# Layer 0's attention: ScalarE squares three of the 22 units of each group of heads a second time itself

## What is computed

```python
def polynomial_attention(q, k, v, degree, is_causal):       # degree = 4
    a = jnp.einsum('bhnd,bhmd->bhnm', q, k) ** degree
    if is_causal:
        a = jnp.tril(a)
    denom = jnp.sum(a, axis=-1, keepdims=True)
    return jnp.einsum('bhnm,bhmd->bhnd', a / denom, v)
```

## Time and profile before

| | us |
|---|---|
| median of 3 runs | 889.47 |
| lowest, highest | 888.18, 890.79 |
| the profiled execution's own time | 884.85 |
| its span, first to last instruction | 883.1 |
| this stage in it, first score to last `read_out0` | 207 to 318 |

### The profile page before, as it was taken

How to read it: one execution, slowest core, us unless ns; L and a number is a source line. 1 busy time by engine, 2 the same in 40 slices (tenths; PEclk the granted TensorE clock), 3 DMA queues, 4 the chain that set the end, 5 groups by cost and what they waited for, 6 DMA issues and landing times.

```text
span 883.1 us, 13675 instructions
## 1 busy us (share of the span) xinstructions
PE 798.7 (90%) x4707; PEld 632.4 (72%) x4707; DVE 621.6 (70%) x1115; ACT 447.9 (51%) x795; POOL 426.8 (48%) x474
## 2 busy tenths in 40 slices
PE   2999999988888866998899899999999999999996
PEld 2866666664223345777889788989999998887874
DVE  8377767458898855888895996767776655555556
ACT  3322231168666723476654656655666653555541
POOL 2466736334655533554532456676773310655550
PEclk9999999997787796999999999999999999999999
DMA  5121195000000004000000001110110477654307
GB/s 176 36 72 36 37 280 134 1 0 1 1 1 1 1 1 140 14 19 12 19 7 19 7 20 42 44 48 25 49 49 14 169 165 283 200 145 114 89 4 236
DMA packets 50114, 59.79 MB, mean 68 GB/s; under 512 B 13559, under 2 KB 41084, under 8 KB 50048
## 3 DMA queue, kind: packets, MB, share of 16 engines
q1 hardware_dynamic: 45488, 50.49, 19.1%
q0 software_dynamic: 4560, 8.44, 2.7%
HBM read 41.11 MB, written 21.86 MB: 71 GB/s over the span
## 4 chain that ended last, share of the span: by engine, by line
PE 71%; DVE 17%; issue 4%; ACT 4%; POOL 3%; DMA 0%; SPq 0%; DVEq 0%; ACTq 0%; POOLq 0%
PE ps L693 11%; PE ps L452 11%; PE ps L454 11%; PE ps L453 10%; PE ps L778 7%; PE ps L596 6%; PE ps L802 3%; DVE A L1245 3%; PE ps L533 2%; DVE swap L1309 2%; DVE cap L1319 2%; PE ps L516 2%; PE ps L491 2%; PE ps L759 2%; DVE qk_tok L1245 1%
## 5 line engine op out<-in xcount | busy, mean ns | idle before, releaser
L693 PE MATMUL ps<-V,P 128*128 128x129 f32 x1152 | 152.8, 279 | 0.0
L993 ACT ACTIVATE cap<-cap 128x1024 f32<-128x1024 f32 (+7 forms) x128 | 87.1, 680 | 123.6 <-DVE cap L1319 117.2
L693 PEld LDWEIGHTS ps<-V,P 128*128 128x128 f32 x1152 | 145.4, 194 | 2.7
L1319 DVE SCALAR_TENSOR_TENSOR cap<-dist,ps 128x1024 f32<-128x1024 f32 (+7 forms) x128 | 95.1, 749 | 25.6 <-PE ps L454 20.7
L1528 POOL TENSOR_SCALAR_AFFINE_SELECT P<-P 128x128 f32<-128x128 f32 x128 | 38.6, 302 | 149.5 <-ACT P L998 149.2
L1653 POOL DMA_INDIRECT y_scratch<-y_sb,aux_s x63 | 62.0, 984 | 64.5 <-issue 35.2
L998 ACT ACTIVATE P<-cap 128x1024 f32<-128x1024 f32 (+7 forms) x128 | 87.7, 685 | 4.1
L452 PE MATMUL ps<-q_hi,k_hi 128*128 128x512 f32 x192 | 72.2, 376 | 6.5 <-DVE cap L1319 6.2
L1245 DVE TENSOR_TENSOR A<-A 128x1024 f32<-128x1024 f32 (+4 forms) x60 | 63.0, 1104 | 9.0 <-ACT A L942 9.0
L778 PE MATMUL ps<-ew,xT 128*128 128x256 f32 (+1 forms) x252 | 67.2, 389 | 2.1 <-issue 1.2
L889 ACT ACTIVATE e_g<-ps 128x512 f32<-128x512 f32 x32 | 19.1, 597 | 96.7 <-PE ps L454 96.7
(11 more groups left out here) (265 smaller groups left out, 2022.1 us busy)
## 6 DMA issues: line engine op xcount, KB each, us to landing
xg_scratch<-blank SPq DMA_DIRECT2D x1, 8127.0 KB, 32.6
xa<-xg_scratch SPq DMA_DIRECT2D x63, 128.0 KB
ew<-in_experts SPq DMA_DIRECT2D x3, 1920.0 KB, 7.5
ew<-in_experts SPq DMA_DIRECT2D x2, 2688.0 KB, 9.7
y<-y_scratch SPq DMA_DIRECT2D x8, 512.0 KB, 5.8
pk<-in_packed SPq DMA_DIRECT2D x8, 384.0 KB, 3.0
pks<-in_scales SPq DMA_DIRECT2D x8, 384.0 KB, 3.9
wqk<-in_wqk SPq DMA_DIRECT2D x20, 128.0 KB
```

Of the source, the lines that this page charges most:

```text
L693: last = pe.matmul(ps[:, 4 + r % 2, o:o + D1 + 1], P1[:, h % 2, a:a + P], V1[:, j, h // REP, :], start=(j == 0), stop=(j == t))
L993: act.activation(cap[:, n % 2, 0:w], cap[:, n % 2, 0:w], ACT.Tanh, scale=1.0 / (CAP * float(D1) ** 0.5))\
L1319: dve.scalar_tensor_tensor(out=cap[:, n % 2, 0:w], in0=dist[:, 0:w], scalar=slope, in1=psf[:, 1024 * (n % 2):1024 * (n % 2) + w], op0=ALU. ...
```

## The change

Of each row with four units, in rows 0, 1 and 2 of each group, the last unit (heads 2-3, right half: units 3, 7 and 11) has its second square on ACT instead of DVE, as a `Square` activation in place in SBUF. ACT issues it right behind the first square of the following unit. It has a semaphore of its own, `s0_four_act`, for which `out0` waits besides `s0_four`; the thresholds count the units of each engine. The units with the diagonal stay on DVE, so POOL's waits alter only in their number. The first squares, the matmuls, the masks and all transfers are as before.

```diff
+ON_ACT0 = [u[2] > 0 and u[1][0] == 2 and u[0] % NT < 3 for u in UNITS0]
+BY_ACT0 = [sum(ON_ACT0[:n + 1]) for n in range(len(UNITS0))]
+BY_DVE0 = [n + 1 - BY_ACT0[n] for n in range(len(UNITS0))]
...
-                pe.wait_ge(s0_four, DONE0[R])
+                pe.wait_ge(s0_four, BY_DVE0[DONE0[R] - 1])
+                pe.wait_ge(s0_four_act, BY_ACT0[DONE0[R] - 1])
                 pe.wait_ge(s0_mask, MASKED0[R])
...
                 act.activation(dst, src, ACT.Square).then_inc(s0_sq, 1)
+                if n >= 1 and ON_ACT0[n - 1]:
+                    act.wait_ge(s0_sq, n)
+                    act.activation(A0_unit(n - 1), A0_unit(n - 1), ACT.Square).then_inc(s0_four_act, 1)
...
-                dve.wait_ge(s0_sq, n + 1)
-                a = A0_unit(n)
-                dve.tensor_tensor(a, a, a, ALU.mult).then_inc(s0_four, 1)
+                if not ON_ACT0[n]:
+                    dve.wait_ge(s0_sq, n + 1)
+                    a = A0_unit(n)
+                    dve.tensor_tensor(a, a, a, ALU.mult).then_inc(s0_four, 1)
...
-                pool.wait_ge(s0_four, n + 1)
+                pool.wait_ge(s0_four, BY_DVE0[n])
```

More of the change, by code:

```diff
@@ L323, in build_program @@
         qk_ready, stk_hi, stk_ready, stk_ps = sem("qk_ready"), sem("stk_hi"), sem("stk_ready"), sem("stk_ps")
-        s0_ps, s0_sq, s0_four, s0_mask = sem("s0_ps"), sem("s0_sq"), sem("s0_four"), sem("s0_mask")
+        s0_ps, s0_sq, s0_four, s0_four_act, s0_mask = (sem("s0_ps"), sem("s0_sq"), sem("s0_four"), sem("s0_four_act"),
+                                               sem("s0_mask"))
         o0_used, o0_copied, o0_turned, o0_ready = sem("o0_used"), sem("o0_copied"), sem("o0_turned"), sem("o0_ready")
```

## The result

| | before | after |
|---|---|---|
| median of 4 executions each, us | 888.83 | 897.5 |
| lowest, highest | 883.16, 890.79 | 895.31, 902.21 |
| ratio, 95% interval | | 1.0122 [1.0086, 1.0159] |
| again, 23 and 6 executions: medians | 887.0 | 893.87 |
| ratio, 95% interval | | 1.0093 [1.0057, 1.0129] |

The change makes the kernel about 1% slower. The forecast was 895.4 us, in a range of 888 to 903.

The account below looks back on a forecast made before the run. The prediction took the loop of ACT and PE, rather than DVE's busy time, to set the pace where DVE keeps up: +4.0 us over four groups plus 1.9 for the clock, on 889.47, gives 895.4 us, range 888.0 to 903.0.

Parts of the forecast that it names:

- The bound: In the four-group stage, the loop of ACT and PE sets group 2's pace; DVE, 90% busy, bounds group 1.
- The work moved: Three second squares in each group go from DVE to ACT: 13 us off DVE, 10.4 us onto ACT in all.
- Unit 7 at 0: Its second square, 0.86 us behind first square 8, is absorbed by ACT's 1.47 us wait before unit 10.
- Unit 11 at 0.76 in a group: Its second square behind first square 12 delays unit 15's scores on PE; nothing absorbed, +0.76 us.
- Unit 3 at 0.7 to 1.0: Its 0.97 us second square behind first square 4 delays PE's buffers; at most 0.29 us absorbed before unit 8.
- The loop's growth: The loop of ACT and PE gets 1.4 to 1.7 us longer, say 1.6 us, in each group.
- What a lighter DVE gives back: At group ends, ACT's wait before unit 21 shrinks: 1.6 us counted back in group 0, 0.8 in group 1.
- Group by group: Cost without low-clock effects: 0 in group 0, +0.8 in group 1, +1.6 each in groups 2 and 3.
- The clock: PE, fed more slowly in rows 0 to 3, loses clock in one group of four: +1.9 us, bounds 0 to +7.6.
- The sum: For the whole kernel, 4.0 us plus 1.9 us of low clock makes +5.9 us, giving 895.4 us.
- What would show it: Profile signs in the stage: DVE's waits for ACT grow from 9.0 to about 25 us, group 1 exceeds 26.5 us.
- Rival 3: Slowly fed PE keeps the clock low into rows 3 to 5, in all four groups: +11.6 us, 901; chance 0.22.

Follow-up runs that it names:

- The two half changes: Against the kernel before: units 3, 7 and 11 without any second square, ratio 0.9981; DVE unchanged with three extra idle-data squares on ACT, ratio 1.0057.
- ACT's load alone: Kernel before, DVE keeping all its second squares, plus three squares of the same lengths on idle data on ACT: ratio 1.0057, 894.43 against 887.44 us.
- the better versions: Kernel before with second squares on ACT of unit 19; 17 and 19; 7 and 19; or 7, 17 and 19: ratios 0.9915, 0.9892, 0.9896, 0.9890.
- the kernel with units 17 and 19: Kernel before with the second squares of units 17 and 19 on ACT, each right behind its own first square: ratio 0.9892, 876.34 us.

## Why the prediction was right, and which term was wrong

- **The bound.** Right. ACT's idle time was not free, since ACT stands in PE's loop; DVE's 90% was not the bound. The two half changes show both. The prediction's list of ACT's waits leaves out 0.72, 1.12 and 0.31 us before units 16, 18 and 20, which recur in every group from group 1 on; nothing of the change falls into them, but unit 17's square does, in the runs with it.
- **The work moved.** Right: the new squares took 1.05 to 1.09, 0.94 and 0.84 us where 1.06, 0.95 and 0.85 were taken from layer 1's rows, and ACT has 9.6 us more in the stage for 10.4 predicted, DVE 14.3 less for 13.
- **Square by square.** Unit 7 at 0: measured -1.1 with DVE's small relief in it, and the wait before unit 10 is 0.84 us shorter as forecast (0.86). Unit 11 at 0.76 in a group: 0.74 in the profile. Unit 3 at 0.7 to 1.0: 0.94. The loop's growth, 1.6 in a group or 6.4, against +6.5 for ACT's load alone.
- **What a lighter DVE gives back.** This is the term that was wrong: 1.6 in group 0 and 0.8 in group 1, 2.4 together. By itself the relief is worth 0.7 ±0.6 us, and inside the change nothing that can be measured (+6.3 and +7.4 with it, +6.5 without). Two things were misread. The first is that the 3.33 us before unit 21 in group 0 were taken as DVE's lateness. They stand behind the `out0` of row 4, first before the change, then with ACT's load alone, where DVE has all its 22 squares:

```profile
230.19 1.90 PE L533 MATMUL ps<-A,V 128*32 128x512 f32 x8 [1.83 <-POOL A L1598]
```

```profile
229.37 1.06 PE L539 MATMUL ps<-A,V 128*32 128x512 f32 x8 [0.83 <-POOL A L1610]
```

  The wait for the mask is 1.0 us shorter; the other 1.1 of the 2.1 us by which ACT waits less (1.24 instead of 3.33) are this `out0` and the scores behind it at the full clock, where the kernel before had a stretch at 1.2 GHz from 230.3 to 233.7. Whether DVE's lateness brings this stretch, no run separates. The second is that what is saved before unit 21 partly comes back behind it: in group 1, at the full clock before and with unit 11 alone on ACT, the wait before unit 21 is 0.81 us shorter and the next group's first unit follows 0.50 us later, so 0.3 is left of the 0.8. And where the longer ACT loop sets the pace, DVE is no longer late even with all its squares, so there is no more for a lighter DVE to give back.
- **Group by group.** Here the agreement is partly luck. Forecast without the clock were 0, +0.8, +1.6 and +1.6 us. From first square 0 to the next group's, and in group 3 to its unit 21, the profiles have 26.49 and 26.47, 25.83 and 29.60, 27.73 and 27.94, 22.92 and 27.31: 0, +3.8, +0.2 and +4.4. The low clock in them changed by -3.5, +5.7, -2.3 and +6.9 us. The sum, +8.4 for 6.8 us more of low clock, leaves 6.3 at 0.30; which group pays was not foreseen.
- **The clock.** +1.9 predicted. Against the 86 us of before, the changed kernel has 98 and 89 us at 1.2 GHz in its two runs, which at 0.30 are +3.6 and +0.9. The 1.9 lies between them, by a price that was about right: 1.9 us for 7 us of low clock is 0.27 for each. That it would be one group of four was not right: groups 1 and 3 have more of it, 0 and 2 less.
- **The sum.** Predicted 4.0 + 1.9 = 5.9; measured 6.9 us by the medians of the second run and 8.7 by the first. The relief made the forecast 2.4 us too low; without it the sum would be 8.3, between growth and clock of the second run (6.3 + 0.9) and those of the first (7.4 + 3.6).
- **What would show it.** DVE's waits for ACT at A0, the 9.0 of before, grew to 24.0, near the 25 named (with `qk_tok` 11.6 grew to 33.9). PE's wait before the scores of unit 7 in group 1, none before, is 1.01 us, and that before unit 15's grew by 0.85. The wait before unit 21 is 0.34 us in groups 1 to 3, but 1.24 in group 0, where 0.34 was named too. Group 1 takes 29.6 us, over 26.5. Rival 3 had a part: groups 1 and 3 went from 0.86 to 0.77 and from 0.84 to 0.75 of the clock and lost 3.8 and 4.3 us.

## What to carry to other kernels

An engine's idle time can be filled for nothing only where the engine that it waits for is late with work of its own; where the two wait for each other in a loop over a double buffer, every microsecond put into the loop comes out at the end. Ask it of each wait singly: here one of three equal-looking squares was free and two cost their full length. Work on the idle engine paid here where it shortened the chain that everybody waits for, even if that chain is short, and 13 us of relief for a busy engine that does not set the pace was worth under 1 us. Before an idle stretch is put down to a late engine, look at the clock in it: of one wait of 3.33 us a third was the clock.

## What the runs showed of the hardware that I had not expected

- Executions of one kernel in one setting spread over 9 us, and the time at 1.2 GHz goes with most of it: slope 0.30, scatter 0.9 us over 193 executions. It also counts between kernels: of the 8 to 11 us that the better versions gain, between 4 and 7 came with 15 to 23 us less of low clock. One profile can mislead by that much, as the one of before did, which was among those with the least.
- Which kernel gets the better clock was not foreseen. Unit 11 alone on ACT had 69 to 74 us at 1.2 GHz in all twelve executions, the kernel before 72 to 101. Why a square that lengthens the loop goes with a better and steadier clock stays open; no run takes it apart.
- POOL's mask of 128x256 takes as long as the square that DVE does beside it, and 0.41 us when DVE has none: in the kernel before it is 1.33, 1.20, 1.07 and 0.93 us beside squares of 1024, 896, 768 and 640 elements, which take 1.28, 1.16, 1.03 and 0.88. In the kernel with units 17 and 19 the two masks of row 5, during which DVE is in `read_out0` on PSUM, took 0.80 us for both. The first row below is a mask beside a square, the second these two:

```profile
247.98 0.94 POOL L1614 TENSOR_SCALAR_AFFINE_SELECT qk_tok<-qk_tok 128x256 f32<-128x256 f32 x1 [0.74 <-DVE qk_tok L1259]
...
251.71 0.80 POOL L1614 TENSOR_SCALAR_AFFINE_SELECT A<-A 128x256 f32<-128x256 f32 x2 [0.88 <-DVE A L1259]
```

  In the kernel before, unit 19's mask fell beside unit 20's square and took 1.33 us (285.23 in group 2), so 0.92 us of the shorter chain is the mask. This may be why unit 19 gains more than its own length; no run takes it apart. The Trainium skill ("SBUF — State Buffer", Who interferes with whom) says that a DVE instruction with two inputs in SBUF contends with a GpSimd instruction that reads SBUF, over ports that the two share as an exclusive lock. The rows agree with it.
